# Second gather stage of a graph network: a ring of ten slots, gathers without index copies, table adds one turn behind

## The chip, the cores and the metric

The kernel runs on one core of one Trainium2 chip. The metric is the device time of one execution in microseconds (us). One execution was also taken by the hardware profiler; its trace is what the sections below read. Engines are named as in the profile: PE is TensorE (matmuls), PEld its weight loads, DVE is VectorE, ACT is ScalarE, POOL is GpSimd, SP is SyncE, which here only issues DMA transfers.

## What is computed

There are 12,500 nodes of 64 features and 400,000 edges with 64 attributes each, sorted by their target node. Two graph layers run, each followed by a residual add and a layer norm. The first layer sends each edge's source row and attributes through a matrix, a batch norm and a SiLU, and averages over the target. The second layer, in which the change lies, is:

```python
msg = relu(x1[src] + edge_attr)                    # 400,000 x 64
agg = segment_sum(msg, dst, num_segments=12500)
h   = (1.0 + eps) * x1 + agg
x2  = layernorm(x1 + relu(h @ W.T + b))
```

Here x1 is the output of the first layer, 12,500 x 64 in fp32. It lies in DRAM (x1_scratch), and its rows are fetched by `src`, which is random.

## The kernel before

**Tiling.** A group is 640 edges: 128 partitions times TG = 5 edges. There are G = 625 groups. S = 5 groups make a turn, SB = 125 turns. The edge attributes of a group come in one DMA of 160 KB (SP, L1138); the rows of x1 come in five indirect DMAs, the gathers, each of 128 rows of 256 bytes (POOL, L1156), with the row numbers read from SBUF. So the stage has 3125 gathers.

**Stages.** In order: preparation; a first gather stage over all groups (lines 328 to 555, gathers in L349); a pass over what it stored (563 to 687); node work (855 to 1111); the second gather stage, lines 1116 to 1221, which is the one that changes; a general version of it that is skipped unless a flag is set (1224 to 1314); and the final linear layer and norm (1319 to 1387).

**The second gather stage.** Buffers E (edge attributes), X (gathered rows), msg and hot have five slots each, one for each group s of a turn. For one group the work runs so:

- POOL waits until the row numbers of the group stand in slot s of `idx_ring` (idx_ready) and until slot s of X has been read (sum_ready), and issues five gathers.
- DVE makes the one-hot tile `hot` (L1202), which says for each edge which of 48 neighbouring nodes it goes to. It waits for the edge attributes and the gathers, and adds them into E (L1208, the edge sum). It copies the row numbers of the group five ahead from `src_idx` into `idx_ring` (L1211). It waits for PE's `summed`, and adds the result in PSUM to the table of sums at the window of this group (L1216, the table add).
- ACT applies the ReLU, E to msg (L1171).
- PE multiplies msg by hot into PSUM, five matmuls in the program, which the trace shows as ten (L1185). It alternates between two PSUM banks and waits for the table adds two groups back.
- SP reloads slot s of E when ACT has read it.

**What sets the order.** Nothing reorders the program: each engine runs its own instructions in the order in which they stand, and the engines meet by semaphores alone. `reuse(engine, sem, n)` is a wait that is left out in turn 0. The first turn stands by itself, the rest is a loop over turns on each engine. DVE's order in a turn is: one-hot, edge sum, index copy, table add of group 0, then the same of group 1, and so on. At the start of each turn `load_windows` (L166) reads five window positions into registers, and the dynamic slices `ds(firsts[s], WIN)` use them. `loop_halves(engine, first, end, turn)` (L34) is a helper, there already for the pass before, that loops over pairs of turns, so that each half of a ring of ten has fixed addresses.

## Time and profile before

| | us |
|---|---|
| median of 3 runs | 10885.92 |
| lowest and highest run | 10885.71, 10889.72 |
| span of the profiled execution | 10892.7 |
| stages ahead of the second gather stage | 0 to 6110 |
| second gather stage | 6110 to 10780 |
| final layer and norm | 10780 to 10893 |

Times in the trace are microseconds from the start of the span, unless ns is said. A row of the timeline gives start, duration, engine, line, operation, output and inputs, count, and in brackets how long the engine had sat idle before it and what the profile holds to have ended that. "issue" is idle time for which the profile sees no wait. "remote" is a wait whose releaser it did not find. "remote" and a DMA are put down as releasers by what came last in the trace, so with a table add (L1216), whose instruction waits for PE alone, such a name does not say what was waited for. Ends of matmuls are modelled.

### The profile page before, as it was taken

The page shows a single profiled execution, that of the slowest core. Times are in us where ns is not written, and L with a number is a line of the kernel's source. Part 1 is how long each engine was busy: PE and PEld are TensorE (multiplying, and loading weights), DVE is VectorE, ACT ScalarE, POOL GpSimd, SP SyncE. Part 2 cuts the span into 40 slices and gives each one's busy share as a digit, 9 for nine tenths or more (in the row PEclk, how much of TensorE's full clock was granted, in tenths as well). Part 3 has the DMA queues.
Part 4 walks back from the last instruction along what each step waited for, and adds up shares of the span by engine and source line. Part 5 has one row for each costly group of instructions (what it writes and reads, how often), then busy time and mean ns, then how long its engine had stood idle before and what let it go on. Part 6 is the DMA issues. An engine that isn't in the chain of part 4 may idle for free. (4 is left out here: it accounts for less than half of the span.)

```text
span 10892.7 us, 119855 instructions
## 1 busy us (share of the span) xinstructions
PE 4140.9 (38%) x36713; PEld 3322.5 (31%) x36713; DVE 2557.8 (23%) x7060; ACT 1173.7 (11%) x2055; POOL 6799.3 (62%) x6897
## 2 busy tenths in 40 slices
PE   4445444444444445445887311111111111111113
PEld 3333333333333333334776211111111111111112
DVE  2111111111111111114997311111111111111112
ACT  0000000000000000001334300000000000000001
POOL 5555555555555555556998466666666666666663
PEclk7655555656665655555555555555555555555555
DMA  2222222222222222222443111111111111111111
GB/s 78 60 61 61 61 61 60 61 61 61 61 61 61 61 60 61 61 61 75 125 123 114 50 44 44 43 45 44 44 44 44 44 43 45 44 43 45 44 44 35
DMA packets 882270, 637.83 MB, mean 59 GB/s; under 512 B 534579, under 2 KB 780831, under 8 KB 881496
## 3 DMA queue, kind: packets, MB, share of 16 engines
q1 hardware_dynamic: 590300, 326.49, 10.9%
q0 software_dynamic: 200416, 208.55, 10.2%
q10 hardware_dynamic: 91536, 102.58, 2.7%
q8 instruction: 8, 0.13, 0.0%
q14 instruction: 10, 0.08, 0.0%
HBM read 528.19 MB, written 108.90 MB: 58 GB/s over the span
## 5 line engine op out<-in xcount | busy, mean ns | idle before, releaser
L349 POOL DMA_INDIRECT Z<-in_x_dram,idx_ring x3125 | 2958.8, 947 | 2088.3 <-DVE idx_ring L526 1205.2
L1156 POOL DMA_INDIRECT X<-x_scratch,idx_ring x3125 | 2986.5, 956 | 1738.3 <-issue 893.5
L1185 PE MATMUL PS<-hot_c,msg_c 128*64 128x48 f32 x6250 | 811.6, 310 | 3865.8 <-ACT msg_c L1171 2630.0
L1185 PEld LDWEIGHTS PS<-hot_c,msg_c 128*64 128x64 f32 x6250 | 713.5, 223 | 3964.0 <-issue 2528.7
L401 PE MATMUL PS<-ZT,W_sb 128*64 128x256 f32 x2500 | 689.5, 647 | 2375.0 <-ACT ZT L451 2238.9
L515 DVE BATCH_NORM_STATS2 stats<-PS 128x320 f32 (+1 forms) x625 | 311.6, 499 | 3158.2 <-remote 2670.5
L1216 DVE TENSOR_TENSOR table<-table,PS 64x48 f32 x625 | 130.0, 208 | 3773.0 <-remote 1822.2
L401 PEld LDWEIGHTS PS<-ZT,W_sb 128*64 128x64 f32 x2500 | 183.7, 199 | 2637.2 <-ACT ZT L451 2488.9
L451 ACT ACTIVATE ZT<-PS 128x640 f32<-128x640 f32 x625 | 439.4, 703 | 4602.4 <-remote 4300.2
L391 PE MATMUL PS<-ident,Z 128*128 128x128 f32 x3125 | 845.7, 413 | 161.7 <-issue 158.6
L420 PE MATMUL PS<-W_sb,ZT 128*64 128x64 f32 x12500 | 877.7, 318 | 0.0
L605 POOL TENSOR_TENSOR normed<-normed,shift 128x320 f32<-128x320 f32 x625 | 823.8, 1356 | 46.1 <-DVE normed L652 46.1
L1171 ACT ACTIVATE msg_c<-E 128x320 f32<-128x320 f32 x625 | 293.1, 469 | 4380.9 <-DVE E L1208 2271.7
L420 PEld LDWEIGHTS PS<-W_sb,ZT 128*64 128x64 f32 x12500 | 761.0, 223 | 0.0
L633 PE MATMUL PS<-hot,msg 128*64 128x48 f32 x6250 | 658.0, 293 | 174.9 <-ACT msg L618 92.8
L633 PEld LDWEIGHTS PS<-hot,msg 128*64 128x64 f32 x6250 | 630.4, 211 | 202.7 <-issue 172.8
L391 PEld LDWEIGHTS PS<-ident,Z 128*128 128x128 f32 x3125 | 551.7, 210 | 267.9 <-issue 191.7
L522 DVE TENSOR_TENSOR h_ring<-PS,b_row 128x320 f32<-128x320 f32 x625 | 303.6, 486 | 851.7 <-remote 802.7
L652 DVE TENSOR_TENSOR normed<-h_turns,scale 128x640 f32<-128x640 f32 x375 | 369.5, 986 | 17.4 <-DMA h_turns<-h_scratch 5.6
L403 PEld LDWEIGHTS PS<-ZT,W_sb 128*64 128x64 f32 x2500 | 300.4, 226 | 220.9 <-issue 215.8
L618 ACT ACTIVATE msg<-normed 128x320 f32<-128x320 f32 x625 | 293.8, 470 | 534.6 <-POOL normed L605 525.2
L1208 DVE TENSOR_TENSOR E<-X,E 128x320 f32<-128x320 f32 x625 | 302.4, 484 | 23.2 <-DMA X<-x_scratch,idx_ring 21.4
(140 smaller groups left out, 2682.9 us busy)
## 6 DMA issues: line engine op xcount, KB each, us to landing
Z<-in_edge_attr_dram SPq DMA_DIRECT2D x625, 160.0 KB
h_scratch<-h_ring ACTq DMA_DIRECT2D x625, 160.0 KB
h_turns<-h_scratch SPq DMA_DIRECT2D x125, 800.0 KB
E<-in_edge_attr_dram SPq DMA_DIRECT2D x625, 160.0 KB
Z<-in_x_dram,idx_ring POOLq DMA_INDIRECT x3125
X<-x_scratch,idx_ring POOLq DMA_INDIRECT x3125
x_nodes<-in_x_dram SPq DMA_DIRECT2D x1, 3125.0 KB
x_ring<-in_x_dram SPq DMA_DIRECT2D x25, 125.0 KB
```

The source lines that it names most:

```text
L349: nc.gpsimd.indirect_dma_start(out=Z[:, s, j, 0:D], out_offset=None, in_=x, in_offset=bass.IndirectOffsetOnAxis(ap=idx_ring[:, s, j:j + 1] ...
L391: last = nc.tensor.transpose(banks(rows_at, 2, P, EG)[:, j * P:(j + 1) * P], Z[:, s, j, :], ident[:, :])
L401: nc.tensor.matmul(h[lo:lo + D, 0:2 * P], W1_sb[:, :], ZT[:, half * 2 * P:(half + 1) * 2 * P], start=True, stop=True)
L420: last = nc.tensor.matmul(PS[lo:lo + D, 6 + s % 2, j * D:(j + 1) * D], ZT[:, j * P + lo:j * P + lo + D], W1_sb[:, :], start=True, stop=True)
L451: act.activation(ZT[:, :], banks(2 * (s % 2), 2, P, EG), ACT.Copy).then_inc(zt_taken, 1)
L515: nc.vector.bn_stats(stats[:, ds(i * (6 * S) + 6 * s, 6)], PS[:, 4 + s % 2, 0:HC]).then_inc(stats_done, 1)
L522: nc.vector.tensor_tensor(h_ring[:, s, :, :], PS[:, 6 + s % 2, 0:HC].rearrange("p (t c) -> p t c", c=D), b1_row[:, :].unsqueeze(1).to_broa ...
L605: nc.gpsimd.tensor_tensor(rows, rows, shift1[:, :].unsqueeze(1).to_broadcast([P, TG, D]), ALU.add).then_inc(shifted, 1)
L633: last = nc.tensor.matmul(PS[D:P, s, 0:WIN], msg[:, s, j, :], hot[:, half, s * TG + j, :], start=(j == 0), stop=(j == TG - 1))
L652: nc.vector.tensor_tensor(normed[:, half, a * TG:b * TG, :], h_turns[:, half, a:b, :].rearrange("p g (t c) -> p (g t) c", c=D), scale1[:, ...
L1156: nc.gpsimd.indirect_dma_start(out=X[:, s, j, :], out_offset=None, in_=x1_dram, in_offset=bass.IndirectOffsetOnAxis(ap=idx_ring[:, s, j:j ...
L1185: last = nc.tensor.matmul(PS[D:P, s % 2, 0:WIN], msg[:, s, j, :], hot[:, s, j, :], start=(j == 0), stop=(j == TG - 1))
```

## The change

The second gather stage alone is rewritten.

- The ring has ten slots (RING = 10): two halves of five, one for each parity of the turn. E, X, msg, hot and the semaphores of loads and gathers have ten slots; the others become single counters over all groups.
- The gathers take their row numbers straight from `src_idx[:, n:n + 1]`. With that `idx_ring`, its copies on DVE and its semaphores go from this stage. POOL has no loop any more: all 3125 gathers are written out, and group g waits for the edge sum of group g - 10.
- DVE adds the PSUM result of group g - 5 to the table after the edge sum of group g. The five adds of the last turn come after its loop.
- PE uses five PSUM banks, one for each s, and waits for the add of group g - 5. ACT waits for the matmuls of group g - 10 before it overwrites msg, and so does DVE before hot.
- SP loads ten slots of E ahead, then x_nodes, then loops. SP, ACT, PE and DVE run their loops by `loop_halves`.

The diff, cut to its core:

```diff
             with nc.Block() as block:
@@ SP @@
-                            reuse(sp, msg_ready[s], i)
-                            sp.dma_start(E[:, s, :, :], edge_v[i * S + s]).then_inc(e_loaded[s], 16)
+                            r = half * S + s
+                            if later(i):
+                                sp.wait_ge(msg_ready, i * S + (s + 1 - RING))
+                            sp.dma_start(E[:, r, :, :], edge_v[i * S + s]).then_inc(e_loaded[r], 16)
@@ POOL @@
-                    pool.wait_ge(idx_first, 1)
-                            reuse(pool, idx_ready[s], i)
-                            reuse(pool, sum_ready[s], i)
+                    for g in range(G):
+                        r = g % RING
+                        if g >= RING:
+                            pool.wait_ge(sum_ready, g + 1 - RING)
                             carry_wait(pool)
-                                    out=X[:, s, j, :], out_offset=None, in_=x1_dram,
-                                    in_offset=bass.IndirectOffsetOnAxis(ap=idx_ring[:, s, j:j + 1], axis=0)
+                        for j in range(TG):
+                            n = g * TG + j
+                                out=X[:, r, j, :], out_offset=None, in_=x1_dram,
+                                in_offset=bass.IndirectOffsetOnAxis(ap=src_idx[:, n:n + 1], axis=0)
@@ ACT @@
-                            act.wait_ge(sum_ready[s], i + 1)
-                            reuse(act, summed[s], i)
+                            act.wait_ge(sum_ready, i * S + s + 1)
+                            if later(i):
+                                act.wait_ge(summed, i * S + (s + 1 - RING))
@@ PE @@
-                            pe.wait_ge(msg_ready[s], i + 1)
-                            pe.wait_ge(hot_ready[s], i + 1)
-                            reuse(pe, added, i * S + max(s - 1, 0))
+                            pe.wait_ge(hot_ready, i * S + s + 1)
+                            pe.wait_ge(msg_ready, i * S + s + 1)
+                            if not isinstance(i, int) or i >= 1:
+                                pe.wait_ge(added, i * S + (s + 1 - S))
-                                last = nc.tensor.matmul(PS[D:P, s % 2, 0:WIN], msg[:, s, j, :], hot[:, s, j, :],
+                                last = nc.tensor.matmul(PS[D:P, s, 0:WIN], msg[:, r, j, :], hot[:, r, j, :],
@@ DVE @@
-                    nc.vector.tensor_copy(idx_flat, src_idx[:, 0:S * TG]).then_inc(idx_first, 1)
-                            nc.vector.tensor_copy(idx_ring[:, s, :],
-                                                  src_idx[:, ds(i * (S * TG) + (S + s) * TG, TG)]
-                                                  ).then_inc(idx_ready[s], 1)
-                            dve.wait_ge(summed[s], i + 1)
+                    def turn(i, half, n):
                         firsts = windows_of_turn(dve)
                         for s in range(S):
+                            if s == S - 1:
+                                load_windows(dve, i)
+                            one_hot(i, half, s)
+                            edge_sum(half, s, n)
+                            add(i - 1, s, firsts[s])
+
+                    load_windows(dve, 0)
+                    for s in range(S):
+                        one_hot(0, 0, s)
+                        edge_sum(0, s, 0)
+                    turn(1, 1, 0)
+                    loop_halves(dve, 2, SB, turn)
+                    for s, first in enumerate(windows_of_turn(dve)):
+                        add(SB - 1, s, first)
```

The order of the built program shows it at two places. The first is POOL at the stage's gathers, with the rows of before (-) and of the change (+); X is the gathered tile, x_scratch is x1 in DRAM:

```order
-L1147 UNCONDITIONAL_BRANCH
-L1156 DMA X<-x_scratch,idx_ring 128x64 x25
-L1162 UNCONDITIONAL_BRANCH
-L1156 DMA X<-x_scratch,idx_ring 128x64 x25
-L1162 REGISTER_ALU
-L1162 COMPARE_AND_BRANCH
...
+L1150 UNCONDITIONAL_BRANCH
+L1159 DMA X<-x_scratch,src_idx 128x64 x3125
```

A first turn of 25 and a loop of 25 gathers have become one straight piece of 3125, which reads src_idx.

The second place is DVE in its loop, from the one-hot of the first group on, before the change. ISA and REGISTER_ALU are instructions of the sequencer alone (addresses, waits):

```order
L1202 TENSOR_TENSOR hot_c<-window,rel 128x240
L1206 ISA
L1207 ISA
L1208 TENSOR_TENSOR E<-X,E 128x320
L1211 ISA
L1211 COPY idx_ring<-src_idx 128x5
L1214 REGISTER_ALU
L1216 ISA
L1216 TENSOR_TENSOR table<-table,PS 64x48
```

And the same place after it:

```order
L1201 TENSOR_TENSOR hot_c<-window,rel 128x240
L1208 ISA
L1209 ISA
L1210 TENSOR_TENSOR E<-X,E 128x320
L1214 ISA
L1217 ISA
L1217 TENSOR_TENSOR table<-table,PS 64x48
```

The copy between edge sum and table add is gone, and the table add (L1216, now L1217) is that of the group five back, which the rows don't show.

## Rows read from the trace of the kernel before

**Rows 1.** Stretches: busy us of each engine (instructions), granted clock, DMA share, GB/s.

```profile
6110.00:10780.00 4670.00, 811.58 (x6250) 713.54 (x6250) 690.10 (x2500) 293.15 (x625) 2986.49 (x3125) 0.50 0.20 45
```

**Rows 2.** Costliest groups, 6110 to 10780: busy us, mean ns | idle before, releasers.

```profile
L1156 POOL DMA_INDIRECT X<-x_scratch,idx_ring x3125 | 2986.5, 956 | 1738.3 <-issue 893.5 <-DVE idx_ring L1211 751.7 <-DVE idx_ring L1195 73.1
...
L1208 DVE TENSOR_TENSOR E<-X,E 128x320 f32<-128x320 f32 x625 | 302.4, 484 | 23.2 <-DMA X<-x_scratch,idx_ring 21.4 <-issue 1.8
...
L1202 DVE TENSOR_TENSOR hot_c<-window,rel 128x240 f32<-128x240 f32 x625 | 256.2, 410 | 182.3 <-issue 166.5
L1216 DVE TENSOR_TENSOR table<-table,PS 64x48 f32 x625 | 130.0, 208 | 3773.0 <-remote 1822.2 <-DMA Z<-in_edge_attr_dram 1053.8 <-PE PS L1185 554.6
```

**Rows 3.** The line L1156: ns min/median/max, first and last start; idle before it.

```profile
L1156 POOL DMA_INDIRECT X<-x_scratch,idx_ring x3125: 941/944/1249, 6110.0 to 10760.8; - x196
...
  DVE idx_ring L1211: 751.7, 201
```

**Rows 4.** Timeline 8000 to 8050, a turn in the middle of the stage.

```profile
8013.72 0.94 POOL L1156 DMA_INDIRECT X<-x_scratch,idx_ring  x1 [6.02 <-DVE idx_ring L1211]
...
8019.62 1.30 PE L1185 MATMUL PS<-hot_c,msg_c 128*64 128x48 f32 x10 [1.83 <-ACT msg_c L1171]
...
8022.31 0.21 DVE L1216 TENSOR_TENSOR table<-table,PS 64x48 f32 x1 [3.24 <-PE PS L1185]
...
8022.62 1.15 POOL L1156 DMA_INDIRECT X<-x_scratch,idx_ring  x1 [0.30 <-issue]
...
8023.99 1.30 PE L1185 MATMUL PS<-hot_c,msg_c 128*64 128x48 f32 x10 [3.06 <-issue]
8024.08 0.94 POOL L1156 DMA_INDIRECT X<-x_scratch,idx_ring  x1 [0.30 <-issue]
...
8032.23 0.21 DVE L1216 TENSOR_TENSOR table<-table,PS 64x48 f32 x1 [8.79 <-DMA Z<-in_edge_attr_dram]
...
8033.77 0.41 DVE L1202 TENSOR_TENSOR hot_c<-window,rel 128x240 f32<-128x240 f32 x1 [1.33 <-issue]
...
8035.23 1.29 PE L1185 MATMUL PS<-hot_c,msg_c 128*64 128x48 f32 x10 [9.95 <-issue]
...
8044.08 0.95 POOL L1156 DMA_INDIRECT X<-x_scratch,idx_ring  x1 [0.30 <-issue]
8049.06 0.21 DVE L1216 TENSOR_TENSOR table<-table,PS 64x48 f32 x1 [14.38 <-remote]
```

**Rows 5.** Timeline 10755 to 10778, the stage's end.

```profile
10756.78 0.21 DVE L1216 TENSOR_TENSOR table<-table,PS 64x48 f32 x1 [10.85 <-DMA Z<-in_edge_attr_dram]
...
10760.82 0.95 POOL L1156 DMA_INDIRECT X<-x_scratch,idx_ring  x1 [0.30 <-issue]
...
10766.85 1.30 PE L1185 MATMUL PS<-hot_c,msg_c 128*64 128x48 f32 x10 [5.76 <-ACT msg_c L1171]
10768.31 0.21 DVE L1216 TENSOR_TENSOR table<-table,PS 64x48 f32 x1 [1.93 <-PE PS L1185]
...
10777.68 0.21 DVE L1216 TENSOR_TENSOR table<-table,PS 64x48 f32 x1 [2.00 <-PE PS L1185]
```

**Rows 6.** Timeline 6141 to 6163, near the stage's start.

```profile
6141.87 1.31 PE L1185 MATMUL PS<-hot_c,msg_c 128*64 128x48 f32 x10 [4.69 <-issue]
...
6159.03 0.94 POOL L1156 DMA_INDIRECT X<-x_scratch,idx_ring  x1 [0.30 <-issue]
6162.85 0.21 DVE L1216 TENSOR_TENSOR table<-table,PS 64x48 f32 x1 [21.45 <-remote]
```

**Rows 7.** Timeline 2074 to 2081, in the first gather stage.

```profile
2074.14 0.41 PE L408 MATMUL PS<-hot_a,ones_bf 128*64 128x48 bf16 x4
...
2077.84 0.58 PE L391 MATMUL PS<-ident,Z 128*128 128x128 f32 x2 [1.27 <-issue]
...
2080.13 0.50 DVE L515 BATCH_NORM_STATS2 stats<-PS 128x320 f32 x1 [8.19 <-remote]
2080.37 0.70 ACT L451 ACTIVATE ZT<-PS 128x640 f32<-128x640 f32 x1 [7.40 <-remote]
```

More of the change, by code:

```diff
@@ L1116, in gnn_kernel, with later @@
         with ExitStack() as here:
-            E = sb(here, "E", [P, S, TG, D])
-            X = sb(here, "X", [P, S, TG, D])
-            msg = sb(here, "msg_c", [P, S, TG, D])
-            hot = sb(here, "hot_c", [P, S, TG, WIN])
-            e_loaded = sems("c_e_loaded")
-            gathered = gathered_x1
-            sum_ready = sems("sum_ready")
-            idx_ready = sems("c_idx_ready")
-            hot_ready = sems("c_hot_ready")
-            msg_ready = sems("c_msg_ready")
-            summed = sems("c_summed")
+            RING = 2 * S
+            E = sb(here, "E", [P, RING, TG, D])
+            X = sb(here, "X", [P, RING, TG, D])
+            msg = sb(here, "msg_c", [P, RING, TG, D])
+            hot = sb(here, "hot_c", [P, RING, TG, WIN])
+            e_loaded = [sem(f"c_e_loaded{r}") for r in range(RING)]
+            gathered = gathered_x1
+            sum_ready = sem("sum_ready")
+            hot_ready = sem("c_hot_ready")
+            msg_ready = sem("c_msg_ready")
+            summed = sem("c_summed")
             added = sem("c_added")
-            idx_first = sem("idx_first")
             x1_kept = sem("x1_kept")
+            def later(i):
+                return not isinstance(i, int) or i >= 2
             with nc.Block() as block:
@@ L1193, in _, with one_hot @@
+                    turn(0, 0, 0)
+                    turn(1, 1, 0)
+                    loop_halves(pe, 2, SB, turn)
                 @block.vector
                 def _(dve):
-                    nc.vector.tensor_copy(idx_flat, src_idx[:, 0:S * TG]).then_inc(idx_first, 1)
-                    def turn(i):
-                        load_windows(dve, i)
+                    def one_hot(i, half, s):
+                        if later(i):
+                            dve.wait_ge(summed, i * S + (s + 1 - RING))
+                        nc.vector.tensor_tensor(
+                            hot[:, half * S + s, :, :], window[:, :].unsqueeze(1).to_broadcast([P, TG, WIN]),
+                            rel5[:, ds(i * S + s, 1), :].rearrange("p a t -> p (a t)").unsqueeze(2)
+                            .to_broadcast([P, TG, WIN]), ALU.is_equal).then_inc(hot_ready, 1)
@@ new lines, in edge_sum, with add @@
+                    def edge_sum(half, s, n):
+                        r = half * S + s
+                        dve.wait_ge(e_loaded[r], n * 16 + 16)
+                        dve.wait_ge(gathered[r], n * (16 * TG) + 16 * TG)
+                        nc.vector.tensor_tensor(E[:, r, :, :], X[:, r, :, :], E[:, r, :, :],
+                                                ALU.add).then_inc(sum_ready, 1)
+                    def add(i, s, first):
+                        dve.wait_ge(summed, i * S + s + 1)
+                        if not isinstance(i, int) or i * S + s > 0:
+                            dve.wait_ge(added, i * S + s)
+                        nc.vector.tensor_tensor(table[D:P, ds(first, WIN)], table[D:P, ds(first, WIN)],
+                                                PS[D:P, s, 0:WIN], ALU.add).then_inc(added, 1)
```

55 lines of the change are left out of this document (16 added, 39 removed).

## The prediction

> **What bounds the kernel now.** Three views, from coarse to fine. The table of stretches gives the second gather stage 4670 us of the 10892.7 us span; in it POOL is busy 2986 us, DVE 690, PE 812, ACT 293, and the DMA engines a fifth of the time [rows 1]. No compute engine is near its limit, so the reader looks at POOL, which issues the 3125 gathers one behind the other. The costliest groups show its row: 956 ns a gather on average against a median of 944, and before the gathers 1738.3 us of idle time, which falls into "issue", the index copy of DVE (L1211) and one wait of 73.1 us for the stage to begin [rows 2, 3]. The timeline says how the idle time is made. Between 8024.08 and 8044.08 POOL starts a gather every 1.25 us, 16 in a row, so 0.306 us of gap behind each median gather belongs to issuing; then nothing until the next turn, and the same pause stands in the turn before as 6.02 us at 8013.72, released by DVE's index copy [rows 4]. In all, 751.7 us of the idle time end with that copy [rows 3].
>
> The copy is late because DVE is late. In DVE's order it stands behind the edge sum of its own group, and that behind the table add of the group before. At 8035.23 PE runs ten matmuls in 1.29 us, to 8036.52, yet the add that needs them starts at 8049.06 after 14.38 us of idle DVE; the group before waits from 8023.99 + 1.30 = 8025.29 to 8032.23 [rows 4]. The data for the next sum had landed long before: DVE waits in front of the sum (L1208) only 23.2 us in the whole stage, in front of the add (L1216) 3773 us [rows 2]. So POOL waits for a sum that waits for an add that waits for PE's signal, and the signal comes 7 to 13 us after the recorded matmuls. When POOL is through, signals come at once: matmuls at 10766.85 + 1.30, add at 10768.31 [rows 5]. At the stage's start POOL issues without pause, the matmuls of 6141.87 are followed by an add only at 6162.85, 2.9 us after POOL's last gather before it ended (6159.03 + 0.94) [rows 6]. I read this as: while POOL issues gathers, PE's signals can be held back. Why, the trace does not say.
>
> **The change, part by part.** (1) *Ring of ten, no index copy.* The gathers of group g now wait only for the sum of group g - 10, and nothing else. (2) *Adds one turn behind.* DVE's order becomes one-hot g, sum g, add g - 5. A signal held for group p stops DVE behind the sum of p + 5, hence POOL in front of the gathers of p + 16. When the matmuls of p end, POOL is in group p + 1, so the signal may be some 14 to 15 groups late, 14 x 6.3 = 88 us, before POOL notices. The longest wait of DVE in front of an add that any row shows is 21.45 us [rows 6]. So the pauses should go, and what is late next is POOL's own issuing.
>
> The sum for POOL. Before, first start 6110.0 to last end 10760.82 + 0.95: 4651.8 us [rows 3, 5]. After, without pauses: 2986.5 busy + 3124 gaps x 0.306 = 3942.4 us [rows 2, 4]. Saved: 709 us. That is 6.31 us a group against 7.44.
>
> The tail. From POOL's last end to the end of the last add (10777.68 + 0.21) pass 16.1 us, five groups of 3.1 us one behind the other [rows 5]. After, four of these five are summed while POOL still issues; left are the landing, one sum-to-add chain of some 3 us and five adds of 0.24 us: I take 8 us, so 8 saved (between 0 and 11).
>
> The start. The copy in front of the first gather goes, 1 us at most saved. SP issues ten edge loads ahead of the load of the nodes (x_nodes) instead of five; POOL needs none of them, DVE's first sums come no later than the gathers land, and POOL is ten groups (63 us) ahead of the first sum that it waits for. Nothing.
>
> Costs. *DVE*: one copy less a group (625 x 0.166 = 103 us, was beside POOL's pause), else the same instructions, 587 us of 3943. It is hidden behind the gathers; its work a group, about 1.3 us with gaps, must stay under 6.3. *PE and ACT*: the same work; PE now waits for the add of g - 5, ACT for the matmuls of g - 10, both five groups or more back. *PSUM*: five banks by turns in place of two, no cost. *Code*: POOL's loop of 25 gathers becomes 3125 in a row with the wait instruction per group kept; the trace shows no such stretch. Below: nothing, since the first 40 gathers, 6110.0 to 6159.03, and the 25 of a turn, 8013.72 to 8044.08, keep to 1.26 us each [rows 3, 4, 6]. Above: the dearest turn boundary that the trace shows is DVE's, 1.33 us before L1202 at 8033.77 [rows 4]; once per 25 gathers that is 125 x 1.33 = 166 us. I take nothing, since the straight pieces are the nearest rows to what POOL will run; a gain is excluded because the gap of 0.306 us stands inside them already. *Gathers beside DVE*: a gather takes 1.15 us instead of 0.94 where it begins under a DVE operation (8022.62) [rows 4]; the sum of this is in the mean already (3125 x 12 ns = 37 us). DVE's sum, add and one-hot now follow each landing closely, at the same phase every time: between none (37 us less) and one gather of each group (625 x 0.21 = 131, so 94 us more). I keep the 37.
>
> Together 709 + 8 + 1 = 718 us off the profiled 10892.7. The profiled execution is 6.8 us over the median of the runs, 10885.92, so I forecast **10,168 us**.
>
> One rule of the Trainium skill speaks against so smooth a stage. The row first: 1250 DVE operations with both inputs in SBUF (one-hot 410 ns, sum 484 ns) cost the gathers 37 us in all, 0.03 us each [rows 2, 3]. "SBUF — State Buffer", section "Who interferes with whom", says that such an operation contends with a GpSimd instruction that reads SBUF and that the later one blocks fully. Where each of them held a gather for its whole length, that would be 625 x 0.894 = 559 us in place of 37; this is rival D.
>
> **The rivals.** *B: held signals come only when POOL pauses.* Then POOL runs 15 groups past the held one, pauses, everything is delivered, and PE and DVE catch up by n groups until signals are held again. A cycle takes 6.31 n + 5.7 us (the pause of rows 4 without its gap). Pause and the prompt start behind it last some 10 us, 7 groups of PE's 1.3 us: 7.12 us a group, 625 x (7.44 - 7.12) = 200 us saved, 10,686 us. With n = 15 it is 6.69 and 10,415; with n = 5, 7.45 and no change. For it: the adds at 8049.06 and 6162.85 come where POOL has stopped. Against: the add at 8032.23 came with POOL in full run, and so did the add at 10756.78, with POOL issuing until 10760.82; and in the first pass two signals of PE work recorded at 2074.14 and 2077.84 reach DVE and ACT at 2080.13 and 2080.37 together, so one release delivers all that is due [rows 4, 5, 6, 7].
>
> *C, slower: PE itself is slow under the gathers, and becomes the bound.* If not the signal but the work is held, PE serves a group in the time from its matmuls to the add: 2.7 us (8019.62 to 8022.31), 8.2 (8023.99 to 8032.23) and 13.8 us (8035.23 to 8049.06), 8.3 on average [rows 4]. POOL without pauses offers a group every 6.31 us; PE would take 625 x 8.3 = 5188 us, 536 us more than 4652: 11,420 us. It turns slower than before from 7.44 us a group on. Beside it the skill's "Perfetto Trace Analysis", section "Tensor Engine Instruction (MATMUL, LD_WEIGHTS)", fits: the recorded end of a matmul is an estimate, not an observation. Against: the two signals 0.24 us apart in the first pass, from work recorded over 3 us apart, with other matmuls of 0.58 us in it [rows 7].
>
> *D: the DVE operations hold every gather that they meet.* 559 - 37 = 522 us of the gain are lost: 10,690 us. *E: the change doesn't loosen the chain*, because the late sum comes from something else that the add's row only stands for (an edge load, a landing): 10,885 us. Against it, the 23.2 us before L1208.
>
> **How the numbers follow.** A, POOL's issuing alone: 0.80. B 0.11, C 0.04, D 0.03, E 0.02. A by itself reaches from 10,168 - 37 - 8 = 10,120 to 10,168 + 94 = 10,262, with a part of the code's 166 us to about 10,330. The range goes on to the mild end of B, 10,415, and leaves out the rest: 10,110 to 10,420. A measurement of this kernel tells 0.2%, some 22 us, from no change. Faster by more than that: A, D and nearly all of B, 0.93; within it: E and the n = 5 end of B, 0.02; slower: C and the worse side of B (n below 5), 0.05.
>
> **What the profile after would show.** POOL's row: 3125 gathers, some 956 ns, idle before them near 950 us plus the wait for the stage, almost all "issue", and no releaser from DVE with hundreds of microseconds. The stage from the first gather to the last: 3940 us; over 4100 and B, D or the code is in it. B shows as pauses of 5 us every 45 to 95 us, D as a mean gather of 1.1 us, the code as pauses at even counts of gathers, C as a PE that waits for nothing but itself, with DVE's waits before the add growing. The step most in doubt is that a signal is never held for 88 us; DVE's longest wait before L1217 tells it. Wrong altogether would be this forecast if DVE waits before the sum with gathers long landed.

## The result, and the profile after

The changed kernel takes **10,747.34 us** (median of three, 10,744.88 to 10,748.52) against 10,885.92 before: 0.987 of it, 95% interval 0.985 to 0.989. It is faster, by 139 us where 718 were forecast, and lies outside the range of 10,110 to 10,420.

The stretch of the second gather stage, in the view of [rows 1] (busy us of PE, PE's weight loads, DVE, ACT, POOL with counts; granted clock, DMA share, GB/s):

```profile
6115.00:10640.00 4525.00, 963.01 (x6256) 803.32 (x6257) 640.87 (x1875) 294.67 (x627) 2992.21 (x3125) 0.51 0.20 46
```

The costliest groups, which answer to [rows 2], and the releasers of the gathers' line, which answer to [rows 3]:

```profile
L1159 POOL DMA_INDIRECT X<-x_scratch,src_idx x3125 | 2992.2, 958 | 1585.2 <-issue 986.9 <-DVE E L1210 525.6 <-POOLq L109 72.7
L1188 PE MATMUL PS<-hot_c,msg_c 128*64 128x48 f32 x6250 | 957.8, 282 | 3567.2 <-issue 3537.8 <-ACT msg_c L1172 25.9 <-DVE hot_c L1201 1.4
...
L1210 DVE TENSOR_TENSOR E<-X,E 128x320 f32<-128x320 f32 x625 | 303.0, 485 | 51.0 <-DMA X<-x_scratch,src_idx 32.5 <-issue 18.4
...
L1217 DVE TENSOR_TENSOR table<-table,PS 64x48 f32 x625 | 130.2, 208 | 3731.8 <-DMA shares_scratch<-counts 2483.7 <-PE PS L1188 877.0 <-issue 358.6
```

```profile
L1159 POOL DMA_INDIRECT X<-x_scratch,src_idx x3125: 942/947/1272, 6115.8 to 10619.5; - x196
...
  issue: 986.9, 3044
  DVE E L1210: 525.6, 80
```

A gather costs what it did, 958 ns against 956. The 751.7 us behind DVE's index copy have become 525.6 us behind its edge sum: POOL still pauses. In numbers worked out from the gathers' starts and lengths, with every gap over 1 us called a pause, the kernel before has 134 pauses of 753.6 us in all, the changed one 92 of 586.4; half of the stretches between them are of 45 gathers or more, where 25 was the most before, but for the first 40. The stage from first start to last end falls from 4651.8 us to 10,619.5 + 0.9 - 6115.8 = 4504.6. It starts 5.8 us later than before (6115.8 for 6110.0): the first gather stage, which the change leaves alone, took that much longer.

PE's row is new in kind: 3537.8 of its 3567.2 us of idle time are "issue", time in which it waited for nothing that the profile shows. The timeline shows what that is (start, length, engine, line, operation, count, idle before). A stretch in the middle of the stage, POOL running, then a pause:

```profile
8000.81 0.24 PE L1188 MATMUL PS<-hot_c,msg_c 128*64 128x48 f32 x1 [2.55 <-issue]
...
8002.21 0.18 PEld L1188 LDWEIGHTS PS<-hot_c,msg_c 128*64 128x64 f32 x1 [2.62 <-issue]
...
8003.61 0.24 PE L1188 MATMUL PS<-hot_c,msg_c 128*64 128x48 f32 x1 [2.56 <-issue]
...
8013.54 0.21 DVE L1217 TENSOR_TENSOR table<-table,PS 64x48 f32 x1 [26.26 <-DMA shares_scratch<-counts]
...
8016.10 0.95 POOL L1159 DMA_INDIRECT X<-x_scratch,src_idx  x1 [5.24 <-issue]
...
8021.11 0.95 POOL L1159 DMA_INDIRECT X<-x_scratch,src_idx  x1 [0.30 <-issue]
...
8024.65 7.14 PE L1188 MATMUL PS<-hot_c,msg_c 128*64 128x48 f32 x68 [0.48 <-issue]
8024.81 0.21 DVE L1217 TENSOR_TENSOR table<-table,PS 64x48 f32 x1 [9.51 <-DMA shares_scratch<-counts]
...
8026.83 1.10 POOL L1159 DMA_INDIRECT X<-x_scratch,src_idx  x1 [4.77 <-DVE E L1210]
...
8032.57 0.13 PEld L1188 LDWEIGHTS PS<-hot_c,msg_c 128*64 128x64 f32 x1 [0.90 <-issue]
...
8033.30 0.20 PE L1188 MATMUL PS<-hot_c,msg_c 128*64 128x48 f32 x1 [1.50 <-issue]
```

While POOL issues, PE's weight loads and matmuls start one by one on a grid of 0.70 us: 8000.81, 8002.21, 8003.61, and again 8032.57, 8033.30. (The step is 0.70 us or a multiple of it: of the intervals between neighbouring PE records of the stage, 1613 are 0.65 to 0.75 us long and 1658 are 1.3 to 1.5 us. No record is missing in between, since all 6250 matmuls are in the trace.) At 8024.65, 2.6 us after POOL's last gather before its pause ended (8021.11 + 0.95), 68 matmuls run in 7.14 us, 0.105 us each, and DVE and ACT follow with a group each 1.1 us; 5.7 us after POOL is back, PE is on the grid again. Twenty PE instructions a group (ten weight loads, ten matmuls) are, at one step each, 20 x 0.70 = 14 us, against 6.31 us in which POOL offers the next group. The records show more: on the grid PE starts one instruction each 1.1 us on average, and from one group's last matmul to the next one's pass 21 us (median of 101, both from 7 us after POOL's return on). Not every pause helps: that of 5.24 us before 8016.10 brought no burst. Of the 92 pauses 61 brought one (twenty PE instructions or more, close together), 6.8 us after POOL's last gather in the median, so the 2.6 us of this one are short.

### The profile page after: what moved, and what is told of

Same layout as the page of the kernel before. It is cut to its first block and busy times, and to the rows that moved or that the text cites. A ratio compares the mean times of both kernels' runs of the same rounds, so it can differ in the third digit from the quotient of the medians.

```text
span 10746.7 us, 119863 instructions
## 1 busy us (share of the span) xinstructions
PE 4292.2 (40%) x36713; PEld 3411.7 (32%) x36713; DVE 2508.2 (23%) x6434; ACT 1174.5 (11%) x2055; POOL 6811.9 (63%) x6897
## 5 line engine op out<-in xcount | busy, mean ns | idle before, releaser
L1159 POOL DMA_INDIRECT X<-x_scratch,src_idx x3125 | 2992.2, 958 | 1585.2 <-issue 986.9
L1188 PE MATMUL PS<-hot_c,msg_c 128*64 128x48 f32 x6250 | 957.8, 282 | 3567.2 <-issue 3537.8
L1188 PEld LDWEIGHTS PS<-hot_c,msg_c 128*64 128x64 f32 x6250 | 802.1, 204 | 3723.2 <-issue 3720.6
L1217 DVE TENSOR_TENSOR table<-table,PS 64x48 f32 x625 | 130.2, 208 | 3731.8 <-DMA shares_scratch<-counts 2483.7
L1210 DVE TENSOR_TENSOR E<-X,E 128x320 f32<-128x320 f32 x625 | 303.0, 485 | 51.0 <-DMA X<-x_scratch,src_idx 32.5
```

The costliest lines, as they stand in the source:

```text
L1159: nc.gpsimd.indirect_dma_start(out=X[:, r, j, :], out_offset=None, in_=x1_dram, in_offset=bass.IndirectOffsetOnAxis(ap=src_idx[:, n:n + 1] ...
L1188: last = nc.tensor.matmul(PS[D:P, s, 0:WIN], msg[:, r, j, :], hot[:, r, j, :], start=(j == 0), stop=(j == TG - 1))
```

## What was tried on the chip

**The state of the argument.** Theory *supply* (formed only after the first four runs; the expectations call it fetch): while POOL issues gathers, the other engines get their instructions slowly, whatever these do. Theory *PE-slow*: only PE's matmuls and weight loads are slow. Theory *signals held*, that of rival B: PE works at full pace and its signals come late. The chips differ, as the runs showed, so each run stands with the kernel before on its own chip.

### Fewer and more PE instructions

*e1_bf16*, the changed kernel with 5 weight loads and 5 matmuls a group:

```
-            msg = sb(here, "msg_c", [P, RING, TG, D])
-            hot = sb(here, "hot_c", [P, RING, TG, WIN])
+            msg = sb(here, "msg_c", [P, RING, TG, D], bf16)
+            hot = sb(here, "hot_c", [P, RING, TG, WIN], bf16)
```

> The changed kernel with the messages and one-hots of the second gather stage kept in bf16 (the messages are rounded, so the sums are less exact): the five matmuls of a group become 5 weight loads and 5 matmuls in place of 10 and 10. Theory PE-slow (rival C by another price): in the changed kernel PE starts an instruction only every 0.70 us while POOL issues gathers (20 instructions, 14 us a group against 6.31 that POOL needs). Ten instructions are 7.0 us, close to POOL's 6.31 us, and with fifteen groups of slack the pauses nearly go: stage 3945 to 4400 us in place of 4505, total 10,190 to 10,640, most likely 10,250. Theory signals-held (rival B): the work on PE is not what takes the time, so the stage stays at 4505 us and the total at 10,747 +- 20.

*e2_one* (changed kernel) and *e4_before_one* (kernel before), one matmul a group, 4 PE instructions, with four of the five tiles left out of the sums; here e2_one's edit, e4's is the same in the other kernel's names:

```
-                            for j in range(TG):
-                                last = nc.tensor.matmul(PS[D:P, s, 0:WIN], msg[:, r, j, :], hot[:, r, j, :],
-                                                        start=(j == 0), stop=(j == TG - 1))
+                            last = nc.tensor.matmul(PS[D:P, s, 0:WIN], msg[:, r, 0, :], hot[:, r, 0, :],
+                                                    start=True, stop=True)
```

> The changed kernel with one fp32 matmul a group in place of five (four of five tiles are left out of the sums), 4 PE instructions a group in place of 20. PE-slow: 4 x 0.70 = 2.8 us a group, well under POOL's 6.31 us; no pauses after stage start, POOL's issuing alone bounds, total near 10,168 (10,150 to 10,220). Signals-held: PE's count of instructions does not matter, 10,747 +- 20.

> The kernel before with one fp32 matmul a group in place of five (four of five tiles left out of the sums), its ring of five, index copies and adds as they were. PE-slow: the matmul-to-add step takes 2.8 us or less in place of up to 14, so the sums and index copies are never late, and the kernel before also comes down to POOL's issuing: 10,170 to 10,300. Signals-held: the same waits of up to 14 us, 10,886 +- 20.

*e3_twice*, the changed kernel with each group's matmuls done twice:

```
+                            for again in (0, 1):
                                 for j in range(TG):
...
```

> The changed kernel with the five matmuls of each group done twice (the second time starts the sum anew), 40 PE instructions a group. PE-slow: 28 us a group while POOL issues; PE gets less done in both the stretches under gathers and the pauses, about 7.9 us a group or more in place of 7.2: 11,180 or more, up to 11,800. Signals-held: PE's pure time a group grows from 1.1 to 2.2 us, beside POOL's 6.31, so no change, or at most a few tens of us: 10,747 to 10,790.

All four ran on one chip, where the kernel before took 10,879.6 us; the ratios are to that, those of the first profile to its own. Pauses are counted as above:

| kernel | PE instructions a group | time, us | ratio to before (95%) | pauses | us in pauses |
|---|---|---|---|---|---|
| before (first profile) | 20 | 10,885.9 | 1 | 134 | 753.6 |
| changed (first profile) | 20 | 10,747.3 | 0.987 (0.985 to 0.989) | 92 | 586.4 |
| e1_bf16 | 10 | 10,641.9 | 0.978 (0.977 to 0.980) | 97 | 487.8 |
| e2_one | 4 | 10,623.1 | 0.977 (0.975 to 0.979) | 157 | 471.4 |
| e4_before_one | 4 | 10,628.5 | 0.977 (0.975 to 0.979) | 171 | 493.8 |
| e3_twice | 40 | 10,885.8 | 1.001 (1.000 to 1.002) | 127 | 740.7 |

Signals held falls: it expected 10,747 for e1, e2 and nearly that for e3. But PE-slow misses too, by hundreds of microseconds: half of PE's instructions away brought 105 us where some 500 were held likely (the run lies 2 us outside the range), four fifths of them 124 us where 580 were expected, and doubling them cost 139 us where 430 or more were expected. With 40 instructions a group PE starts one each 0.74 us on the grid, and not each 1.1 us, so the pace is not fixed; what sets it stays open. And e2_one and e4_before_one are equal within their intervals: with four PE instructions a group, the ring of ten and the adds one turn behind bring nothing measurable. The kernel before holds a second piece of evidence against held signals. From the recorded start of a group's last matmul to its table add, 99 in 100 groups take up to 14.3 us in the kernel before and up to 5.1 us in e4_before_one, which differs only in 4 instructions for 20. (The medians are 1.1 and 3.0 us; it is the long waits that go.) A held signal would not count instructions. The PE records of [rows 4] that show ten matmuls in 1.29 us are therefore read as no measure of when that work was done.

What holds e2_one back is seen in its timeline:

```profile
8024.18 0.21 DVE L1216 TENSOR_TENSOR table<-table,PS 64x48 f32 x1 [4.37 <-issue]
...
8026.97 0.41 DVE L1200 TENSOR_TENSOR hot_c<-window,rel 128x240 f32<-128x240 f32 x1 [2.58 <-issue]
...
8028.36 0.49 DVE L1209 TENSOR_TENSOR E<-X,E 128x320 f32<-128x320 f32 x1 [0.99 <-issue]
...
8032.57 0.21 DVE L1216 TENSOR_TENSOR table<-table,PS 64x48 f32 x1 [3.71 <-issue]
```

With PE out of the way DVE goes the same way. A group takes it 8032.57 - 8024.18 = 8.39 us, twelve steps of 0.70, all of the idle time "issue". The records of DVE's sequencer in between (register operations and semaphore waits, which the views don't count as busy) last 0.70 us each there: 2238 of them between 0.67 and 0.73 us in the stage, none in the kernel before. Nine of the twelve steps hold a record of DVE, so an instruction costs one step or two, a wait as much as a matmul, and it is DVE with 8.4 us that now exceeds POOL's 6.31. That is the supply theory, formed here and tested next.

### Each engine by itself

*m1* and *m2* are measuring programs: POOL issues 64 operations of one kind in a row, and beside it PE, DVE, ACT or SP run straight rows of small instructions that wait for nothing. The core of m1:

```
 nc.gpsimd.indirect_dma_start(out=X[:, n, :], out_offset=None, in_=x, ...)   # POOL, n in range(64)
 nc.tensor.matmul(PS[0:D, 0:48], w[:, :], r[:, :], start=True, stop=True)    # PE, 60 steps of 10, bf16
 nc.vector.tensor_copy(tiny[:, k, :], small[:, :])                           # DVE, 400
 act.wait_ge(put, base + k + 1); act.activation(seen[:, k, :], small[:, :], ACT.Copy)
```

> A measuring program, not the kernel: its output is only a copy of x and everything else is left out. In seven parts, one after the other, PE runs 60 steps of ten small bf16 matmuls (20 PE instructions), ACT one tiny operation behind each step, DVE 400 tiny copies, while POOL does: nothing; 64 indirect gathers of 128 rows; 64 indirect gathers of 16 rows; 64 plain DMAs issued from POOL; 64 elementwise operations; nothing, with 64 loads issued by SP; and again 64 gathers, with PE and DVE in small loops (21 and 8 instructions a turn) in place of straight code. Theory fetch: while POOL issues DMAs that its own software describes, every engine gets its next instruction only each 0.70 us once what it had ahead is used up, so that in parts 2, 3 and perhaps 4 a PE step takes 14 us and DVE's copies fall to one each 0.70 us, PE and DVE alike; ACT, with two instructions a step, stays behind PE by nothing; in parts 1, 5 and 6 a step takes about 1 us and a copy about 0.07 us. In part 7 the loops are either as slow (turns are fetched anew) or at full speed (turns are kept). Theory PE-slow: the steps take 14 us in part 2 but DVE's copies keep their pace. Theory work-on-DVE's-side (contention in SBUF): part 5 slows DVE too.

One stretch of each of m1's parts 2 to 6, in the view of [rows 1]: 128-row gathers, 16-row gathers, plain DMAs issued by POOL, elementwise work on POOL, loads issued by SP.

```profile
110.00:170.00 60.00, 4.36 (x22) 2.80 (x22) 8.66 (x44) 0.41 (x2) 40.11 (x43) 0.50 0.14 24
220.00:270.00 50.00, 3.45 (x18) 2.30 (x18) 6.30 (x35) 0.41 (x2) 33.54 (x40) 0.50 0.02 3
315.00:345.00 30.00, 7.55 (x226) 7.47 (x224) 17.14 (x234) 4.59 (x23) 22.66 (x44) 0.68 0.17 49
360.00:395.00 35.00, 5.43 (x172) 5.33 (x169) 35.00 (x185) 3.70 (x18) 27.70 (x41) 0.60 0.00 1
420.00:450.00 30.00, 11.63 (x312) 11.28 (x309) 15.65 (x221) 5.74 (x28) 3.51 (x4) 0.69 0.25 54
```

Under gathers PE starts 22 + 22 instructions and DVE 44 in 60 us: 1.36 us for one, twice the 0.70 us expected, where 0.07 us a copy is DVE's pace without them (m2_c's 135 copies in 9.66 us below). The pattern is the same for gathers of 16 rows, which move almost nothing (3 GB/s), so neither the bytes nor the number of rows make it. Plain DMAs issued by POOL and loads issued by SP leave both engines at speed; elementwise work on POOL slows DVE, which shares something with it (35.00 us busy for 185 copies), but not by this mechanism, since PE goes on. Part 7, small loops in place of straight code, was as slow on PE: 18 weight loads and 18 matmuls in 50 us. PE's own report by ACT agrees with its records here, two steps of 20 instructions in 60 us.

> A second measuring program, not the kernel (its output is a copy of x, everything else is left out). POOL issues 64 indirect gathers of 128 rows in each of seven parts, beside: (1) PE's bf16 matmuls alone (ACT reports each step of 20 instructions), (2) DVE's tiny copies alone, (3) ACT's tiny operations alone, (4) SP's semaphore instructions alone, (5) PE, DVE and ACT together, (6) DVE's wide copies of about 1 us each alone, (7) ACT alone with a pause of about 4 us in POOL's gathers behind every 16. In the first measuring program PE and DVE together got one instruction each 1.40 us. Theory shared supply (one instruction each 0.70 us for all engines together): 0.70 us an instruction in 1 to 4 (a PE step 14 us), and 2.1 us an instruction for each engine in 5. Theory supply of each engine's own: 1.40 us in 1 to 5. In 6 either theory expects the wide copies to keep their pace of about 1.1 us or go to 1.4. In 7 the instructions held up come in a burst in each pause. Theory PE-slow: only part 1 and PE in part 5 are slow.

> The second measuring program again (its output is a copy of x, everything else is left out), since the chip of the last call showed no slowing at all: there the kernel before took 9052 us. Where the kernel before takes some 10,880 us: theory shared supply, 0.70 us an instruction for PE alone, DVE alone, ACT alone, SP alone, and 2.1 us for each of PE, DVE and ACT together; theory own supply, 1.40 us in all five parts; theory PE-slow, only PE's instructions. Where the kernel before takes some 9050 us: no slowing in any part, copies each 0.07 us, as before.

> The second measuring program once more (its output is a copy of x, everything else is left out), for a chip that slows the instructions. Where the kernel before takes some 10,880 us or more: theory shared supply, 0.70 us an instruction for PE alone, DVE alone, ACT alone, SP alone, and 2.1 us for each of PE, DVE and ACT together; theory own supply, 1.40 us in all five parts; theory PE-slow, only PE's instructions. Where it takes some 9050 us: full pace in every part.

m2 and m2_b fell on a chip (called F here) on which nothing was slow at all: the first line below, DVE alone, 280 copies, the last of its 400, in 20.39 us. m2_c, on a chip where the kernel before takes 11,146 us, has PE alone, DVE alone, ACT alone, then all three together:

```profile
150.00:180.00 30.00, 0.00 (x0) 0.00 (x0) 20.39 (x280) 0.00 (x0) 22.68 (x24) 0.50 0.14 27
```

```profile
85.00:140.00 55.00, 3.95 (x20) 2.55 (x20) 0.00 (x0) 0.41 (x2) 37.38 (x40) 0.50 0.15 25
200.00:250.00 50.00, 0.00 (x0) 0.00 (x0) 7.34 (x39) 0.00 (x0) 32.08 (x34) 0.50 0.13 23
300.00:350.00 50.00, 0.00 (x0) 0.00 (x0) 0.00 (x0) 7.20 (x35) 36.70 (x39) 0.50 0.15 26
...
510.00:570.00 60.00, 4.37 (x22) 2.69 (x21) 8.28 (x43) 8.70 (x43) 41.79 (x45) 0.50 0.14 25
620.00:650.00 30.00, 0.00 (x0) 0.00 (x0) 29.62 (x45) 0.00 (x0) 23.13 (x23) 0.50 0.14 25
```

55 us for 40 PE instructions, 50 for 39 copies (the last few faster, POOL's gathers end at 242.2), 50 for 35 operations of ACT; in all three, and among SP's semaphore instructions in the trace, one each 1.40 us, and the same 1.40 us for each of three engines that run together. It is a supply of each engine's own, and no engine is spared. The last line is 45 of 70 wide copies, one each 0.66 us, the pace that they have on chip F. The part is too short to test anything: DVE alone ran some 80 copies before it fell to its slow pace, so 70 may have been at hand already. That an engine has so many instructions ahead is not shown; beside PE and ACT, DVE fell after 41.

The last part gives the time constants. POOL stops gathering for six elementwise operations; ACT, by then at one or two instructions each 0.7 us or more, is released 3.1 us after POOL turns to them and keeps its full pace for 8 us:

```profile
713.58 4.11 POOL L77 TENSOR_TENSOR big_out<-pool_src 128x256 f32<-128x256 f32 x6
```

```profile
715.98 0.20 ACT L102 ACTIVATE tiny_a<-small 128x4 f32<-128x4 f32 x1 [0.50 <-issue]
716.68 8.00 ACT L102 ACTIVATE tiny_a<-small 128x4 f32<-128x4 f32 x83 [0.50 <-issue]
```

The next two such stops, each behind 16 gathers, released it after 2.9 and 3.0 us. Behind 64 gathers it takes longer: the last gather beside DVE alone ends at 242.2, and the copies are at full pace only from 252.44, though no DMA moved anything from 244 on:

```profile
248.24 0.17 DVE L112 COPY tiny<-small 128x4 f32<-128x4 f32 x1 [1.23 <-issue]
248.94 0.24 DVE L112 COPY tiny<-small 128x4 f32<-128x4 f32 x2 [0.53 <-issue]
...
252.44 9.66 DVE L112 COPY tiny<-small 128x4 f32<-128x4 f32 x135 [0.53 <-issue]
```

So the release is no fixed time: 3 us behind 16 gathers, 10 us behind 64, and in the changed kernel 6.8 us in the median. What was not found is why the measuring programs' engines keep to steps of 1.40 us where PE in the changed kernel and DVE in e2_one take 0.70 and 1.40 about equally often.

### Waits alone

*e5_waits* is e2_one with DVE's two waits in front of a table add written three times; the first of them:

```
-                        dve.wait_ge(summed, i * S + s + 1)
+                        for again in range(3):
+                            dve.wait_ge(summed, i * S + s + 1)
```

> e2_one (the changed kernel with one matmul a group, four of five tiles left out of the sums) with each of the two waits in front of a table add written three times, some 6 to 8 instructions of DVE a group more (12 before), none of which waits for anything that the first didn't. Theory fetch: a group takes DVE 18 to 20 instructions x 0.70 = 12.6 to 14 us while POOL issues, where 8.4 stood; the stage gets slower than e2_one's 4388 us, by 100 to 250 us: total 10,720 to 10,870. Theory PE-slow, or any in which DVE's instructions cost their ordinary 35 ns: under 0.3 us a group more, beside POOL's 6.31: 10,623 +- 15.

It ran on a chip where the kernel before takes 11,155.7 us and gave 10,754.4, 0.965 of it (0.961 to 0.968). Without e2_one on that chip the absolute expectation can't be read; the stage took 4433 us where e2_one's took 4387 on its own chip. Those 46 us are under the 100 to 250 that supply expected, and they may be the chip's: the first gather stage, the same in both, took 5101 us for 5018. The run is **inconclusive**. The trace holds only two more DVE records a group, not the six to eight expected.

### On a chip without the slowing

> The changed kernel, run beside e6_batched and e7_adds_now so that they are compared on one chip: 10,747 us, or 0.987 of the kernel before, on any chip.

> The changed kernel beside them on one chip: 0.987 of the kernel before where PE's instructions are slow under gathers, 0.999 where they are not.

> The changed kernel with DVE's table add of a group directly behind its edge sum again, as in the kernel before; ring of ten and unrolled gathers kept. POOL may then be ten groups ahead of a late add in place of fifteen (five before). If the gain of 139 us comes from fewer, deeper pauses, this lies between: 10,790 to 10,850. If it comes from the ring alone, 10,747 +- 15; if from the adds' order alone, 10,886 +- 15.

> e7_adds_now again (adds not behind, ring of ten and unrolled gathers kept). On a chip that slows the instructions: between the kernel before and the changed one, 0.991 to 0.997 of the kernel before, if fewer and deeper pauses make the gain. On a chip that doesn't: 0.998, as before.

*e7_adds_now* takes one half of the change back, the adds one turn behind; with it the windows are loaded at the turn's start again and the five last adds go:

```
                             one_hot(i, half, s)
                             edge_sum(half, s, n)
-                            add(i - 1, s, firsts[s])
+                            add(i, s, firsts[s])
```

All of these ran on chip F, in two sets. The kernel before took 9052.4 and 9040.8 us there, the changed kernel 9043.9 and 9037.8: ratio 0.999 (0.998 to 1.000) and 1.000 (0.999 to 1.000), no difference. The expectation of 0.987 on any chip (after_again) was wrong, and those of e7_adds_now could not be read here. e7 took 9031.7 and 9024.5, 0.998 both times (0.997 to 0.999), some 13 us better than the changed kernel. The changed kernel's gathers, then its PE and DVE in the middle of the stage:

```profile
L1159 POOL DMA_INDIRECT X<-x_scratch,src_idx x3125 | 2990.2, 957 | 1024.5 <-issue 951.7 <-POOLq L109 72.7
```

```profile
7009.60 0.49 DVE L1210 TENSOR_TENSOR E<-X,E 128x320 f32<-128x320 f32 x1 [5.16 <-DMA X<-x_scratch,src_idx]
7010.12 0.21 DVE L1217 TENSOR_TENSOR table<-table,PS 64x48 f32 x1
...
7010.91 1.30 PE L1188 MATMUL PS<-hot_c,msg_c 128*64 128x48 f32 x10 [5.03 <-DVE hot_c L1201]
```

POOL's idle time is 951.7 us of its own issuing and nothing else: 2990.2 + 951.7 = 3941.9 us from first to last gather, where the forecast had 3942.4. DVE waits for landings, and the add, that of the group five back, starts at once. Of the 1703 us between the changed kernel's 10,747 and its 9044 here, 563 lie in this stage and 1127 in the first gather stage, which the change leaves alone: 3905 us from first gather to last on F, 5032 in the first profile.

### Fewer instructions around the matmuls

*e6_batched* keeps e1's matmuls and makes one one-hot of five groups, sums and Relus of two and three groups, one edge load a turn:

```
+            STEPS = ((0, 2), (2, 5))
...
+                        sp.dma_start(E[:, half, :, :, :].rearrange("p s j c -> p s (j c)"),
+                                     edge_turns[:, ds(i * S, S), :]).then_inc(e_loaded[half], 16)
...
+                        nc.vector.tensor_tensor(E[:, half, a:b, :, :], X[:, half, a:b, :, :], E[:, half, a:b, :, :],
+                                                ALU.add).then_inc(sum_ready, 1)
```

> The changed kernel with the same matmuls as e1_bf16 (messages and one-hots in bf16, messages rounded) and fewer instructions around them: one one-hot of five groups a turn, edge sums and Relus of two and three groups, one edge load a turn, PE's waits twice a turn. By the lists of instructions a turn of ten groups has 44 in place of 70 on DVE, 60 in place of 70 on PE (a matmul counted once), 14 in place of 32 on ACT, 8 in place of 32 on SP. Theory fetch (each instruction costs 0.70 us or more while POOL issues, whatever it does): the stage, 4408 us in e1_bf16, comes down to 4170 to 4330 us, total 10,400 to 10,560, likely 10,480. Theory PE-slow (only matmuls and weight loads are slow): same matmuls, the same 4408 us, 10,640 +- 20, or slower through the coarser steps.

> e6_batched again (messages and one-hots in bf16, messages rounded; fewer instructions around the matmuls). On a chip that slows the instructions under gathers: fetch 10,400 to 10,560 us, or 0.957 to 0.971 of the kernel before (e1_bf16 was 0.978); PE-slow 0.978. On a chip that doesn't: 1.013, as before.

> e6_batched once more (messages and one-hots in bf16, messages rounded; fewer instructions around the matmuls). On a chip that slows the instructions: fetch 0.957 to 0.971 of the kernel before (e1_bf16 was 0.978); PE-slow 0.978. On a chip that doesn't: 1.013.

On chip F it is slower: 9167.7 and 9157.9 us, 1.013 both times (1.011 to 1.015). Its gathers take as much longer, 997 ns on average in place of 957, 124 us in all:

```profile
L1161 POOL DMA_INDIRECT X<-x_scratch,src_idx x3125 | 3114.5, 997 | 1024.5 <-issue 951.8 <-POOLq L109 72.8
```

That one-hots of 1409 ns and sums two and three groups wide hold a gather longer than those of 410 and 484 ns did is the reading; no run lengthened them alone. On a slow chip (kernel before 11,146.4 us) e6 takes 10,774.3, 0.968 (0.965 to 0.970): 46 pauses of 439.6 us, and between them 18 stretches of 150 or 160 gathers and 29 of 10 or 15. The ratio lies in the range of supply and outside PE-slow's 0.978, but that 0.978 was measured on a chip of another kind, and e5_waits reached 0.965 on a chip like this with e2_one's matmul. Neither the changed kernel nor e1 ran on such a chip. So the test that e6 was made for stays **undecided**; what it suggests is that saved instructions and longer DVE operations pull against each other.

### Which half of the change

> e7_adds_now (DVE's table add directly behind its edge sum again; ring of ten and unrolled gathers kept) for a chip that slows instructions under gathers. If the gain of the change is that POOL gets further ahead of a late add, five groups before, ten here, fifteen in the changed kernel, so that the pauses are fewer and each serves more groups: between the two, with 100 to 125 pauses where the kernel before has 134 and the changed kernel 92. If it comes from the ring alone: equal to after_c. If from the order of the adds alone: equal to the kernel before.

> The changed kernel beside e7_c on one chip. Where the kernel before takes some 10,880 us: 0.987 of it. Where it takes some 11,150 us (the chips of the first measuring program and of e6_c), e6_c got 0.968 and e5_waits 0.9645; if a supply of instructions is what is slow there too, the changed kernel gets more than 1.3% there, 0.970 to 0.985.

Both ran on a slow chip (before 10,889.4 us): changed kernel 10,735.8, 0.986 (0.984 to 0.987); e7 10,861.3, 0.997 (0.996 to 0.998). The gathers of e7:

```profile
L1159 POOL DMA_INDIRECT X<-x_scratch,src_idx x3125 | 2968.3, 950 | 1713.4 <-issue 1010.5 <-DVE E L1210 630.1 <-POOLq L109 72.7
```

The ring of ten and the unrolled gathers alone bring 28 us, the adds one turn behind the other 125. The expected count of pauses was wrong, though: e7 has 166 of 738.4 us, more than before, the changed kernel 87 of 580.2 (e7's profile is of its longest run, 10,881.4 us). The ring alone doesn't lengthen the stretches, 20 gathers in the median for 25 before; in e7 DVE still stops on the group that PE has just been given, so PE has no work waiting when a pause sets it free. With the adds behind, several groups lie ready, and one pause serves a burst of them: 68 matmuls at 8024.65. That reading of the difference is argued from the timeline; no run took it alone.

## Why the prediction was wrong

*What bounds the kernel.* Right: POOL waits for a sum, that for an add, that for PE. Wrong, and the step that failed: "I read this as: while POOL issues gathers, PE's signals can be held back." It isn't the signal but the instructions, and not PE's alone. The difference is what scales. A held signal costs a delay that a deeper ring covers; a slow supply costs 0.70 us or more for each instruction of each group, 14 us at one step each and 21 us as measured, against 6.31, and no ring covers a rate. In the sum the step is the term of the pauses: it was put at nothing and measured 586 us. [rows 4] held a hint of it: 2.7, 8.2 and 13.8 us from matmuls to add, on average above 6.31.

*Ring and adds behind.* "A signal is never held for 88 us" was named as the step most in doubt. DVE's longest wait in front of L1217 is 26.9 us, so as a sentence it holds, and yet POOL pauses, since the lags of successive groups add up: the recorded last matmul of a group stands up to 85.5 us ahead of its add, which the order puts behind the sum of the group five on. The waits before the add hardly fell (3773 to 3732 us).

*The sum for POOL.* 3942.4 us was right for a stage without pauses, to a microsecond on chip F. But on F the kernel before shows no loss to win back either (0.999). On the chips with the slowing, which were four of the five that the later runs met and the first one too, 586 us of pauses stand on top.

*Tail and start.* The tail came to 10,632.2 - 10,620.4 = 11.8 us where 8 were taken, 4.3 saved. The start is as forecast, the wait for the stage 72.7 us for 73.1. The profiled spans close with it: 147.2 us of the stage and 4.3 of the tail, less the 5.8 by which it started later, are all but 0.3 us of the 146.0 between 10,892.7 and 10,746.7.

*Code.* Right at nothing: 951.7 us of issuing for 3124 gaps on F is the 0.305 us of a gap in the loop. *Gathers beside DVE.* Right: 958 ns for 956; the 94 us above never came.

*Rival B* had the look of it, pauses of some 5 us (median 6.6) every 45 or more gathers, and its 10,686 us was, with D's 10,690, the nearest; that B came so near is luck, for its mechanism fell with e1, e2 and e3. *Rival C* had the mechanism, and the sign that it was to show: a PE that waits for nothing but itself. It was priced as if a slow PE stayed slow, 11,420 us. In fact POOL's waiting is the cure of what POOL causes, and the loss stays small: even with 40 PE instructions a group the kernel is no slower than the one before. The evidence put against C, the PE records of [rows 7], was worth little, if, as e4 suggests, PE's records stand ahead of the work in kernels where PE waits: by up to 14 us in the kernel before. The Trainium skill's sentence in "Perfetto Trace Analysis", section "Tensor Engine Instruction (MATMUL, LD_WEIGHTS)", that the recorded end of a matmul is an estimate, should have led to doubting that evidence, not only have stood beside the rival; it speaks of ends alone, and by that reading the starts are early too. *Rival D* did not appear in this change (958 ns), but its mechanism may have a price where the operations get longer, the 124 us of e6. *Rival E*, a late edge load or landing, fell with e4_before_one: fewer matmuls alone took the kernel before from 10,879.6 to 10,628.5 us. DVE waited 32.5 us for landings in front of the changed kernel's sums.

The chances were wrong where it matters: B and C together had 0.15, on the evidence of records that no second view confirmed.

**The best version.** e1_bf16 beats both kernels, with messages rounded to bf16: 0.978 of the kernel before on its chip, where the changed kernel had 0.987 and 0.986 on two chips of the same kind. On chip F it wasn't run.

## What to carry to other kernels

Where a stage runs under indirect gathers, count every instruction of every engine, waits and register operations too, and ask whether an engine's count times the mean interval that its records show exceeds POOL's time a group; if it does, hand over more work in one go rather than deepen the ring alone. Read "issue" on an engine with work waiting as a finding, and confirm a matmul's time by the engine that waits for it. A gain that lives on such a loss may exist on one chip and not on another, so compare on several before sizing it.

## What the runs showed of the hardware

- On the chips with the slowing, while POOL issues indirect gathers, PE, DVE, ACT and SP start their instructions on steps of 0.70 us: one each 1.40 us in the measuring programs, alone or together, and in the kernels one each 0.70 or 1.40 us (PE 1.1 us on average in the changed kernel, 0.74 us with its matmuls doubled). In m1 and m2_c it began 2.5 to 7 us after the first gather (DVE alone: first gap at 168.2 us, gathers from 162.6) and ended 3 us after a stop behind 16 gathers and 10 us after one behind 64 (17 us where those had 16 rows). In the changed kernel 61 of 92 pauses ended it, the one shown after 2.6 us, the median after 6.8. Gathers of 16 rows do it as well; plain DMAs from POOL, loads from SP and elementwise work on POOL don't.
- Chips differ in it: the kernel before took 10,880 to 10,889 us on two of the later chips, 11,146 and 11,156 on two others, and 9052 and 9041 us on the fifth, with no trace of it. Which property of a chip decides this is open.
- Doubling the matmuls under such a stage cost 139 us of 10,747, removing four fifths of them gave 124 (run on another chip of the same kind).
